# CIN recommender tower on one core: squares split into three fp32r passes from tile 5 on, tile preparation on other engines

## The reference

```python
B, M, D = 1024, 39, 16; S1, S2 = 128, 128
def _cin_layer(x0, xk, W, b):
    out = jnp.einsum('bhd,bmd,shm->bsd', xk, x0, W) + b[None, :, None]
    return jax.nn.relu(out)
e = jnp.stack([tbl_0[ids[:, 0]], ..., tbl_38[ids[:, 38]]], axis=1)      # (1024, 39, 16)
x1 = _cin_layer(e, e, W1, b1)
x2 = _cin_layer(e, x1, W2, b2)
z = jnp.concatenate([x1.sum(axis=-1), x2.sum(axis=-1)], axis=-1)        # (1024, 256)
h = jnp.concatenate([z, dense_ctx], axis=1)
h = jnp.maximum(h @ W_top1 + b_top1, 0.0)     # 272 -> 512
h = jnp.maximum(h @ W_top2 + b_top2, 0.0)     # 512 -> 256
y = h @ W_top3                                # 256 -> 1
```

## Time and profile before

| | us |
|---|---|
| median of 3 runs | 1227.49 (1227.45 to 1227.75) |
| the profiled execution | 1228.31 |
| its span, first to last instruction | 1226.4 |
| TensorE busy | 1172.4 (96%) |
| VectorE busy | 1005.4 (82%) |
| GpSimd busy | 864.8 (71%) |
| ScalarE busy | 672.1 (55%) |
| mean granted TensorE clock | 0.992 |

### The profile page before, as it was taken

One profiled execution on the slowest core, in us unless ns is written; L12 is line 12 of the kernel. 1 busy time (PEld: TensorE's weight loads), 2 busy tenths in 40 slices (PEclk: granted clock), 3 DMA queues, 4 the chain that ended last, 5 costly groups with the idle time before them and its releaser, 6 DMA issues.

```text
span 1226.4 us, 17749 instructions
## 1 busy us (share of the span) xinstructions
PE 1172.4 (96%) x4784; PEld 879.4 (72%) x4784; DVE 1005.4 (82%) x3692; ACT 672.1 (55%) x2188; POOL 864.8 (71%) x836
## 2 busy tenths in 40 slices
PE   3899999999999999999999999999999999999996
PEld 2577777777777777777776667777777777777775
DVE  4298898888899888888896678888888888887695
ACT  2656666665565656556564465555655565545430
POOL 7888878888888788788776757888886454444350
PEclk9899999999999999999999999999999999999997
DMA  5000000000000000000000000000000000000000
GB/s 177 5 4 4 4 4 3 4 4 5 3 4 3 4 3 3 4 4 3 4 4 3 3 3 3 4 3 4 3 4 2 1 1 1 1 1 1 1 1 1
DMA packets 12801, 9.08 MB, mean 7 GB/s; under 512 B 6190, under 2 KB 11822, under 8 KB 12573
## 3 DMA queue, kind: packets, MB, share of 16 engines
q0 software_dynamic: 10240, 2.64, 2.6%
q1 hardware_dynamic: 2461, 5.31, 1.3%
HBM read 7.92 MB, written 0.00 MB: 6 GB/s over the span
## 4 chain that ended last, share of the span: by engine, by line
PE 72%; DVE 18%; ACT 5%; issue 2%; POOL 2%; DMA 0%; SPq 0%; ACTq 0%
PE ps L724 17%; PE ps L726 17%; PE ps L725 17%; DVE acc L634 15%; PE ps L702 13%; PE ps L690 3%; PE ps L755 3%; ACT e L464 2%; ACT fy L425 2%; POOL looked L339 2%; DVE x1l L595 1%; PE ps L678 1%; DVE e_hl L580 1%; PE ps L697 0%; DVE e_hl L583 0%
## 5 line engine op out<-in xcount | busy, mean ns | idle before, releaser
L634 DVE SCALAR_TENSOR_TENSOR acc<-ps,e,acc 128x128 f32<-128x128 f32 x3200 | 854.4, 343 | 155.7 <-PE ps L726 152.4
L724 PE MATMUL ps<-w2h,x1h 128*128 128x512 f32 (+1 forms) x1280 | 582.4, 455 | 24.9 <-ACT fy L425 13.8
L348 POOL TENSOR_TENSOR fy<-fy 128x512 f32<-128x512 f32 (+1 forms) x256 | 403.0, 1574 | 214.3 <-ACT fy L425 193.5
L425 ACT ACTIVATE fy<-ps,e 128x128 f32<-128x128 f32 x1536 | 418.1, 387 | 198.8 <-PE ps L726 198.3
L726 PE MATMUL ps<-w2h,x1l 128*128 128x512 f32 (+1 forms) x1280 | 495.4, 387 | 0.0
L725 PE MATMUL ps<-w2l,x1h 128*128 128x512 f32 (+1 forms) x1280 | 494.3, 386 | 0.0
L339 POOL DMA_INDIRECT looked<-in_table,rows x320 | 310.9, 972 | 79.1 <-issue 55.0
L724 PEld LDWEIGHTS ps<-w2h,x1h 128*128 128x128 f32 x1280 | 241.5, 189 | 134.1 <-DVE acc L634 50.9
L725 PEld LDWEIGHTS ps<-w2l,x1h 128*128 128x128 f32 x1280 | 241.6, 189 | 82.6 <-issue 44.7
L726 PEld LDWEIGHTS ps<-w2h,x1l 128*128 128x128 f32 x1280 | 240.7, 188 | 48.4
L444 ACT ACTIVATE z<-ps 128x512 f32<-128x512 f32 x192 | 117.9, 614 | 224.8 <-PE ps L690 219.5
(11 more groups left out here) (64 smaller groups left out, 385.5 us busy)
## 6 DMA issues: line engine op xcount, KB each, us to landing
looked<-in_table,rows POOLq DMA_INDIRECT x320, 2.3
w_st<-in_w SPq DMA_DIRECT2D x1, 1728.0 KB, 10.2
wt_sb<-in_wt SPq DMA_DIRECT2D x2, 512.0 KB
w_st<-in_w SPq DMA_DIRECT2D x1, 768.0 KB, 6.3
w_sb<-in_w1a SPq DMA_DIRECT2D x1, 448.0 KB, 3.2
w1b_sb<-in_w1b SPq DMA_DIRECT2D x1, 448.0 KB, 3.8
sel_st<-in_sel SPq DMA_DIRECT2D x1, 234.0 KB
ids_sb<-in_ids SPq DMA_DIRECT2D x1, 150.0 KB, 4.9
```

The costliest lines, as they stand in the source:

```text
L348: nc.gpsimd.tensor_tensor(out, a, b, ALU.add).then_inc(s_fsum, 1)
L425: nc.scalar.activation(fy[:, p % 2, sub, m - MD, :], ps[:, 2 * (nth % RING) + sub, k * S:(k + 1) * S], ACT.Copy, scale=emb(p, sub, m)).the ...
L634: nc.vector.scalar_tensor_tensor(acc[:, sub, :] if m < MD - 1 else y, y, emb(p, sub, m), acc[:, sub, :] if m else fsum[:, p % 2, sub, :], ...
L724: nc.tensor.matmul(y, x1h[:, t % 2, at], w2h[:, cols], start=True, stop=False)
```

## The change

1. **Three fp32r passes.** From tile 5 on (`SOON`), each of the six chunks of squares is split. ScalarE squares the PSUM bank twice, once rounded into `zh` (fp32r), once in float32 back into the same bank. VectorE subtracts (`square_low`) and writes `zl`. TensorE multiplies w1h by zh, w1l by zh and w1h by zl. The bank is free for its next use only when `zl` is there.
2. **Other places for the chunks.** From tile 5 on a chunk is expanded every third slot from slot 6 of the tile on, not every second from slot 11; tiles 2 to 4 differ (one chunk per slot, or every second).
3. **Preparing a tile.** From tile 2 on the sixteen copies are DMAs on SyncE's queue. `multiplied_out` and `low_parts` (the old `products` and `low_part`) run on GpSimd, one tile at a time, in pair 2t - 5 (2t - 4 for tiles 2 to 4). ScalarE's two roundings stay, per tile.
4. **Start.** VectorE's first D banks come in between A banks, and in pairs 0 to 3 (`LATE`) `fsum` is added at the end of the pair, not at its start. GpSimd issues eight lookups in each of these pairs. w1h, w1l and part of w2h are made ahead of the loop.
5. **MLP.** The second group has 448 examples, not 384, and goes at tiles 30/31; 64 examples are left for the end. The MLP's steps are more evenly spaced.

```diff
+SOON = 5
+SPLIT = (0, 1, 2, 3, 4, 5)
+LATE = 4
-LOOKUPS_PER_PAIR = 6
-GROUPS = ((0, 512), (512, 896), (896, 1024))
+GROUPS = ((0, 512), (512, 960), (960, 1024))
@@ bank_order
-    slots = [[("A", 0, a) for a in range(A_BANKS)] + [("A", 1, a) for a in range(EARLY)]]
-    for p in range(PAIRS):
+    slots = [[("A", 0, 0), ("D", 0, 0), ("A", 0, 1), ("D", 0, 1), ("A", 0, 2)]]
+    first = (("D", 0, 2), ("D", 0, 3), ("A", 1, 0), ("D", 0, 4), ("D", 0, 5), ("A", 1, 1), ("D", 0, 6), ("A", 1, 2), ("A", 2, 0))
+    slots += [[bank] for bank in first] + [[]]
+    for p in range(1, PAIRS):
@@ layer1_steps
-    t, k = divmod(slot - 11, TILE_SLOTS)
-    t += 2
-    return [(t, k // 2)] if t < TILES and k % 2 == 0 and k // 2 <= C1 and slot >= 11 else []
+    for t in range(2, TILES):
+        at = TILE_SLOTS * (t - 2)
+        first, apart = (15, 1) if t == 2 else (at + 11, 2) if t < SOON else (at + 6, 3)
+        v, rest = divmod(slot - first, apart)
+        if rest == 0 and 0 <= v <= C1:
+            return [(t, v)]
+    return []
+def is_split(t, v):
+    return t >= SOON and v in SPLIT
+def split_after(p, j):
+    slots = [s for s, kind in enumerate(ORDER) if kind == "D"] + [SLOTS]
+    return [at for s in range(slots[j], slots[j + 1]) for at in layer1_steps(p, s) if is_split(*at)]
+def split_pair(t):
+    return 2 * t - 4 if t < SOON else 2 * t - 5
+SPLIT_IN = {split_pair(t): t for t in range(2, TILES)}
@@ turn_step
-    t = p // 2 + 2
-    return t if p % 2 == 1 and s == 0 and t < TILES else None
+    t = SPLIT_IN.get(p - 1)
+    return t if t is not None and s == (3 if t == 2 else 0 if t < SOON else 4) else None
+def lookups(p):
+    return 8 if p < 4 else 6
@@ SyncE
+                for t in range(FIRST_TILES, TILES):
+                    sp.wait_ge(s_look[t], 16 * LOOKUPS)
+                    for k in range(Q):
+                        for q in range(Q):
+                            sp.dma_start(*put_in_place(t, k, q)).then_inc(s_put[t - FIRST_TILES], 16)
@@ GpSimd, the loop over pairs
-                    share = LOOKUPS_PER_PAIR
+                    share, mine = lookups(p), SPLIT_IN.get(p)
...
+                        if j == 1 and p and mine is not None:
+                            multiplied_out(nc.gpsimd, mine)
...
+                    if mine is not None:
+                        low_parts(nc.gpsimd, mine)
@@ ScalarE, square
+                    if is_split(t, v):
+                        nc.scalar.activation(zh[:, k % 2, :], src, ACT.Square).then_inc(s_z1, 1)
+                        nc.scalar.activation(src, src, ACT.Square).then_inc(s_sq, 1)
+                    else:
+                        nc.scalar.activation(z1[:, k % 2, :], src, ACT.Square).then_inc(s_z1, 1)
@@ VectorE
+                def square_low(t, v):
+                    k = C1 * t + v
+                    dve.wait_ge(s_sq, splits(t, v))
+                    if k >= 2:
+                        dve.wait_ge(s_mm1, k - 1)
+                    nc.vector.tensor_tensor(zl[:, k % 2, :], ps[:, BK_T, :], zh[:, k % 2, :], ALU.subtract).then_inc(s_zl, 1)
...
-                        if fill is not None and j == 4:
-                            products(fill)
-                        if fill is not None and j == 5:
-                            low_part(fill)
+                        for at in split_after(p, j):
+                            square_low(*at)
...
+                        if p < LATE:
+                            dve.wait_ge(s_fsum, ADDS_PER_PAIR * (p + 1))
+                            dve.wait_ge(s_stt, stt_count(p, D_BANKS - 1) - 3 + sub)
+                            nc.vector.scalar_tensor_tensor(x2, x2, 0.0, fsum[:, p % 2, sub, :], ALU.add, ALU.add).then_inc(s_late, 1)
@@ TensorE, layer1
+                    if is_split(t, v):
+                        nc.tensor.matmul(ps[:, BK_ACC1, :], w1h[:, v, :], zh[:, k % 2, :], start=False, stop=False)
+                        nc.tensor.matmul(ps[:, BK_ACC1, :], w1l[:, v, :], zh[:, k % 2, :], start=False, stop=False)
+                        pe.wait_ge(s_zl, splits(t, v))
+                        mm = nc.tensor.matmul(ps[:, BK_ACC1, :], w1h[:, v, :], zl[:, k % 2, :], start=False, stop=(v == C1 - 1))
```

More of the change, by code:

```diff
@@ L248, in cin_tower @@
         s_look = [sem(f"s_look{t}") for t in range(TILES)]
+        s_put = [sem(f"s_put{t}") for t in range(FIRST_TILES, TILES)]
         s_put_act = sem("s_put_act")
@@ L252, in cin_tower @@
         s_el = sem("s_el")
+        s_el_first = sem("s_el_first")
         s_selr = sem("s_selr")
@@ L532, in _ @@
                             mlp(*step)
-                        if fill is not None and s in (1, 3, 4):
-                            put(fill, (1, 3, 4).index(s), 3)
                         for kind, q, j in BANK_SLOTS[1 + SLOTS * p + s]:
```

246 lines of the change are left out of this document (131 added, 115 removed).

## The result

| | before | after |
|---|---|---|
| time of the runs, median | 1227.75 us (17 runs) | 1229.88 us (17 runs) |
| ratio after/before, 95% interval | | 1.0018 (1.0011 to 1.0025) |
| the profiled execution: time, span | 1228.3, 1226.4 us | 1230.69, 1228.8 us |
| pair 0 / pair 6 / pair 58 start | 56.06 / 160.53 / 1099.85 | 40.20 / 186.11 / 1105.92 |
| a tile in the middle | 35.4 on average | 34.57 |

The changed kernel is 0.18% **slower**, where 1224 us, a little faster, was forecast. The time itself lies just inside the 1218 to 1230 that I had given my own forecast; the direction was wrong. What follows is in the order of the prediction's rows. The busy line, as in the earlier trace rows: VectorE has gone from 82% to 87%, TensorE from 96% to 95% although the span is longer.

The account below looks back on a forecast made before the run. TensorE, 34.9 us per tile, was taken as the bound. From 1228.3: start +25.0, steady tiles -24.3, end -4.7, tail -1.0; median 0.8 lower, GpSimd allowance +1.5: 1224 us, own range 1218 to 1230, 8 in 10 within 1208 to 1244.

Parts of the forecast that it names:

- The start: Up to pair 6: TensorE's turns of tiles 2 to 4 wait for GpSimd's low parts, +25.0 us.
- The steady tile: Pair 6 to 58: a tile takes 34.45 us instead of 35.4, -24.3 us with the first MLP group.
- The walk through the banks: Slot-by-slot reckoning of when each bank starts in the steady tile: 34.35 us new order, 34.25 with old squares.
- The waits of 1.4 us: TensorE's waits per steady tile: slots 11 to 18 for VectorE, slots 18 and 1 for ScalarE.
- The first MLP group: Between pairs 6 and 58: it makes tiles 16 to 18 longer by 19.3 us.
- The end: Pair 58 to the last relu, MLP's second group filling TensorE's room: 107.2 us instead of 111.9, -4.7.
- The tail: Last MLP on 64 examples instead of 128: an estimated -1 us of 14.7.
- GpSimd beside the tile: GpSimd's 34.2 us of work beside a tile of 34.45 costs something now and then: 1.5 us added.
- Slow transfers: Rival: tile copies as DMAs in 16-byte runs come late, 1230 to 1233 us or beyond 1250; chance 0.18.
- No shorter tile: Rival: extra squares and subtractions meet badly in the ring, tile 35.2 and more, 1243 us; chance 0.14.
- A cheaper start: Rival: clock and A banks in time, pair 6 at 177, 1215 us; chance 0.15 together with a shorter tile.
- Passes no cheaper: Rival: three passes take TensorE as long as the float32 one, 0.86 us, time about 1228; chance 0.03.

Follow-up runs that it names:

- Low parts earlier: Changed kernel with GpSimd making the low parts of tiles 2 to 4 ahead of the pair's last field sums; 1220.07 us, ratio 0.9902.
- VectorE prepares tiles 2 to 4 alone: Changed kernel with VectorE, not GpSimd, making products and low parts of tiles 2 to 4 only; 1219.55 us, ratio 0.9890.
- the control: The changed kernel unedited, run again beside the kernel before on another chip; 1235.27 us, ratio 1.0021, tile 34.53.
- the run of the old groups: Changed kernel with the MLP's batch groups as before (512, 384 and 128 columns); 1232.86 us, ratio 1.0006.

## Why the prediction was wrong, point by point

**The start: right.** +25.0 was forecast and +25.6 came. Most rows of the forecast stand within 1.6 us of those of the trace: low parts ready at 80.9, 122.5, 164.8 (80.8, 122.8 and 165.2 as starts of L351), fsum of pair 4 at 141.5 (142.0), pair 6 at 185.5 (186.1). TensorE came to the turn of tile 3 at 115.5, not at 113, so the second and third wait are 7.8 and 4.8 us instead of 9 and 6. After the first wait the matmuls run at the lower clock: the rows of the start are 0.63 long at 82.48 and 82.91 and start 0.43 apart. The granted clock falls to the lower level (1.2 GHz) at 73.4, 117.8 and 165.6 us, during the first two waits and at the end of the third, and stays there until 87.1, 128.1 and 169.0 us, that is for 5.9, 4.8 and 3.4 us of work behind them. At about twice the distance between starts this costs half of each (an estimate), so my 1.7 us was right for the last and about 1 us too little for the others.

```profile
81.91 0.77 PE L797 MATMUL ps<-w2h,x1h 128*128 128x512 f32 x1
82.48 0.63 PE L798 MATMUL ps<-w2l,x1h 128*128 128x512 f32 x1
82.91 0.63 PE L801 MATMUL ps<-w2h,x1l 128*128 128x512 f32 x1
```

"Low parts earlier" and "VectorE prepares tiles 2 to 4 alone" confirm the mechanism by taking it away. Some 9 us of the start over the kernel before are left in both, with different waits in each; what makes them stays open. The new order of the first banks, the late fsum and the eight lookups were never tried alone.

**The steady tile: the failed step.** The walk through the banks gave 34.35 and I took 34.45; it is 34.57 to 34.59 at 26 tiles, 3.5 us. The term that was too small is TensorE's own work, "about 33.0": by the starts it is 33.4. The difference lies in the banks, which I had at 26.6 from 0.227 us a matmul; over ten tiles a matmul of 512 columns starts 0.230 us behind the one before it, and the banks take 27.0. The waits of 1.4 us were not too small: they are 1.15 by the same count. Without splits the walk was short by the same 0.24 (34.25 for 34.49), and there TensorE hardly waits. The differences of the walk held better than its level: two splits -0.30 (measured -0.32), six +0.10 (+0.04 against the control), square 1 alone +0.06 to +0.21 (+0.25). Its conclusion that six passes bring nothing is right, and for the reason given. That I passed by the next question, which of the six bring something, is where 0.5 us per tile was lost, 13 us in the whole. VectorE is busy for 95% between pairs 6 and 58 and waits 1.3 us per tile for banks; 93% and 1 were forecast.

**Around the steady tile.** The first MLP group lengthened its tiles by 20.0 us, not 19.3 (40.5 + 46.7 + 36.6 - 3 x 34.6), 0.7 more. Six waits of VectorE for a second square, 8.5 us together, stand there, at a place that the walk did not cover; how much of the 0.7 they make is open. With the 3.5 that is 4.2 of the 4.8 by which -19.5 misses -24.3. Most of the rest is the first tile behind the start: from pair 6 to pair 8 it takes 35.04.

**The end: too good by 2.2.** 107.2 was forecast, 109.4 measured. The step is the price of the MLP's 22 float32 matmuls, 0.75 each or 16.5 us. That price already held the 64 more columns: the run of the old groups shows 2.3 us for them, and 22 x 0.86 x 64/512 is 2.4. What it left out are the four matmuls with 16 rows (`ctx_sb`) and the change to and from them:

```profile
1159.73 0.91 PE L830 MATMUL ps<-p,wt_sb 128*128 128x448 f32 x2
1160.48 0.92 PE L830 MATMUL ps<-p2t,wt_sb 128*128 128x448 f32 x2
1161.32 1.01 PE L830 MATMUL ps<-ctx_sb,wt1c_sb 16*128 16x448 f32 x2
1162.27 0.50 PE L797 MATMUL ps<-w2h,x1h 128*128 128x512 f32 x1
1162.61 0.40 PE L798 MATMUL ps<-w2l,x1h 128*128 128x512 f32 x1
```

The first takes 0.75, the second 0.84, the third 0.95, and the bank behind them starts its second matmul 0.11 late: 2.65 us for 2.25, four times, so 1.6 us. The other 0.6 is of the size by which the banks of two tiles were too cheap (2 x 0.4, an estimate).

**The tail: right** (-1 forecast, -1.2).

**GpSimd beside the tile: nothing.** I had added 1.5 us for an engine at 34.2 beside a tile of 34.45. The tile is 34.6 while the lookups last and 34.6 after their end at 929 us, so it did not bind. Of 5.9 us that the profiled execution stands above the forecast, 4.8 are the steady part, 2.2 the end, 0.6 the start, less 0.2 of the tail and the 1.5. This allowance paid for something that did not happen and brought the forecast nearer by luck.

**The rivals.** *Slow transfers* fell. An issue takes 0.615 us, not 0.47, and 16 of them with 1.9 us to land put tile 2 in place at 60.3, just before the 60.5 from which it would have cost time. The queue's 159901 packets took 7.3% of 16 x 1228.8 us; in the kernel before, without these transfers, the same queue had 2461 packets in 1.3%, so the runs of 16 bytes took about 7.5 ns each. That is under my lower bound of 12. So of the two rules of the Trainium skill that I had cited (DMA: Bandwidth & Descriptors), the one that spares transfers within SBUF from the penalty of small descriptors agrees with this trace. *No shorter tile* fell too: 0.8 us less than the 35.4 of before, where I had 0.95. *A cheaper start* did not come by itself, but came with two lines. *Passes no cheaper* fell: three starts 0.23 us apart.

```profile
581.67 0.39 PE L766 MATMUL ps<-zh,w1h 128*128 128x512 f32 x1
581.89 0.39 PE L767 MATMUL ps<-zh,w1l 128*128 128x512 f32 x1
582.13 0.40 PE L769 MATMUL ps<-zl,w1h 128*128 128x512 f32 x1
582.36 0.39 PE L797 MATMUL ps<-w2h,x1h 128*128 128x512 f32 x1
```

The subtraction forecast at 0.66 to 0.68 has a mean of 0.683. So no mechanism was missing that decides the time. The forecast was a difference of two sums of 25 and 30 us, and an error of a quarter in the one turned the sign: the margin to no change was 3.5 us, and the steady tile alone, with 0.13 us on 26 tiles, took as much.

## What to carry to other kernels

Moving work to an engine with spare time is worth what its place in that engine's queue allows: here two instructions per tile, moved from behind three lookups to ahead of the last additions, gave back 17 us. A cheaper form that hands work to a second engine should be given only to those steps whose place in the row has room on that engine; try it step by step, since six splits brought nothing and four of them 0.5 us per tile. And where a forecast is the difference of two large terms, count the level of the bounding engine from a stretch in which it has no gaps, start to start, before trusting the second decimal of a tile: its busy time showed 0.3 us of idle time per tile where the starts show 1.15 us lost.

## What the runs showed of the chip

- Transfers from SBUF to SBUF in runs of 16 bytes cost about 7.5 ns of a DMA engine each, and their issue on SyncE 0.615 us at the median (0.44 for the load in the earlier trace rows).
- A VectorE operation with both operands in SBUF took 0.21 to 2.8 us beside a busy GpSimd: 0.21 to 0.28 beside the issue of a lookup, and until 0.08 us after its end where it began within an addition. The same on GpSimd took 0.32 each time.
- A float32 matmul of 448 columns cost 0.75 us behind its like and 0.95 with 16 rows; a bank's first matmul after a wait of 0.34 us was followed by the second 0.1 us late.
- ScalarE reads and writes one PSUM bank in place, 512 elements, in 0.617 us, the same as with a destination in SBUF (0.618).
- On three of the five chips ScalarE stood still for 5 to 7 us in the start, in one piece or two, in every kernel whose timeline was read there, and the whole was 5 us longer; the cause stays open.
